# A graph layer's edge step in one round: two octets of tiles, one bank of partial products, one copy, one placing

## The chip, the cores and the metric

The kernel runs on one core of one Trainium2 chip. The metric is the device time of one execution in microseconds (us); lower is better. TensorE (PE) multiplies, VectorE (DVE) and ScalarE (ACT) work on rows, GpSimd (POOL) issues the gathers and scatters that go through an index, and SyncE (SP) issues the plain transfers.

## The reference

There are 12,500 nodes with 256 features and 212,500 edges, sorted by destination, so a node has 17 edges on average.

```
msgs = layernorm(x)[edge_src] * edge_weight[:, None]
agg  = segment_sum(msgs, edge_dst, num_segments=N_NODES)      # sorted
x = x + einsum('ni,oi->no', agg, W) + b
# then a feed-forward part on layernorm(x), with 8 experts:
H = gelu(xf @ W1 + b1);  probs = softmax(H @ Wg + bg);  assign = argmax(probs)
out += where(assign == e, probs[:, e] * (H @ Wd[e] + bd[e]), 0)   # for each e
```

All of it is in float32. The change concerns the sum over edges.

## The kernel before

The kernel has three stages. First the rows of x are normalised and stored to a table in HBM. Then comes the main loop, where nearly all of the time goes. At the end the nodes are sorted by expert, gathered, multiplied by their expert's weights and scattered to the output.

The edges are cut into tiles of 128, and a **step** is 16 tiles. There are 104 steps. GpSimd fetches the source rows with one indirect transfer for each tile (L387), 128 rows of 256 floats, into a ring of three sections of 16 tiles (`xring`). For each tile, VectorE builds a narrow matrix of 32 columns (`sel_narrow`), which has the edge's weight in the column of its destination, counted from the first destination of the tile. A product of that matrix and the fetched rows gives 32 rows of partial sums. Four tiles are a **quad**: their products stand in the four groups of 32 partitions of one bank of PSUM (`psR` or `psG`, in turn; `partial(q)`, L499). VectorE copies the bank to `parts` (L853). A second product with a matrix of zeros and ones (`place`, 64 columns) brings the rows to their places and transposes them (`place_quad(q)`, L507), and VectorE adds the outcome to a window of the sum `agg` in SBUF (`accumulate(q)`, L860). Each of these hand-overs is a semaphore: `s_edge_mm` from the partial products to the copy, `s_parts` from the copy to the placing, `s_placed` from the placing to the addition. So a step has four rounds, which are interleaved.

GpSimd runs ahead and is held back by the ring alone. Section g may be fetched when step g-3 no longer needs it, and this is asked twice for each section:

```
for j in range(STEP_TILES):
    if j % (STEP_TILES // 2) == 0:
        pool.wait_ge(s_edge_mm, g * STEP_TILES + STEP_TILES // 2 + j)
```

The first 8 gathers of a section wait for the first two quads of step g-3, the other 8 for the last two.

When all edges into a group of 512 nodes have been summed, after 4 or 5 steps, a **node group** is worked through: `messages` (L535, product with W, read by VectorE at L919), residual, norm and transposes, and, for the group before, the hidden layer (L557), its gelus on ScalarE (L450), transposes and the rows for the last stage. The order of steps and node groups is a table made on the chip; TensorE and VectorE both loop over it. For a step, VectorE runs `gather_step`, for a node group it runs `first_part` (L907 is its first copy, of `agg`) and `second_part`. There are 25 node groups.

If a tile spans 32 nodes or more, or a quad 64 or more, the step takes another branch (`wide == 1`). None of the 104 steps does with these edges.

## Time and profile before

| | us |
|---|---|
| median of 3 runs | 3659.85 (3650.84 to 3660.72) |
| profiled execution, its own time | 3686.61 |
| its span | 3684.6 |
| TensorE matmuls busy | 2061.4 (56%) |
| VectorE busy | 1151.1 (31%) |
| GpSimd busy | 1822.5 (49%) |
| ScalarE busy | 443.2 (12%) |

The span goes from the first to the last instruction of the profiled execution, and 2.0 us lie around it. A busy time says how much of the span an engine had an instruction in work; no engine is busy all the time here, so what matters is who waits for whom. In the views, PE is the matmuls, PEld the weight loads. A float32 matmul stands as two records, so four tiles show as x8, and the end of a matmul's record is modelled. "remote" is what the view names as the releaser of a wait when no instruction in the profile ended just before it.

### The profile page before, as it was taken

How to read it: one execution, taken by the hardware profiler on the slowest of the kernel's cores; microseconds unless marked ns; L12 is line 12 of the kernel's file. 1: busy time of each engine (PE TensorE's matmuls, PEld its weight loads, DVE VectorE, ACT ScalarE, POOL GpSimd, SP SyncE). 2: the span in 40 equal slices, each digit the busy share in tenths (PEclk: the TensorE clock that was granted, in tenths of full speed). 3: DMA queues.
4: the chain of work that ended last, by engine and by line, in shares of the span. 5: the costliest groups of instructions: out<-in, count | busy, mean ns of one | idle time of the engine just before them, and what ended most of it. 6: DMA issues, size and time to landing. Idle time of an engine off the chain costs nothing.

```text
span 3684.6 us, 40719 instructions
## 1 busy us (share of the span) xinstructions
PE 2061.4 (56%) x10526; PEld 1319.5 (36%) x10527; DVE 1151.1 (31%) x3507; ACT 443.2 (12%) x847; POOL 1822.5 (49%) x1988
## 2 busy tenths in 40 slices
PE   0134555455535554455445544555355548599998
PEld 0112332233323332233223322332233324488887
DVE  8121332233323332233223322332133224733332
ACT  5000000000000000000000000000000002043343
POOL 1656445644565445544664455444644540055554
PEclk9995666566656666566656656666566658799999
DMA  8323332333333332333233323332333231455554
GB/s 358 88 82 98 97 103 84 115 99 98 104 91 106 100 101 83 113 100 101 84 115 100 102 81 111 98 102 86 105 103 100 82 92 63 154 180 180 181 184 139
DMA packets 153598, 420.31 MB, mean 114 GB/s; under 512 B 33320, under 2 KB 67499, under 8 KB 150880
## 3 DMA queue, kind: packets, MB, share of 16 engines
q0 software_dynamic: 100032, 300.27, 27.6%
q1 hardware_dynamic: 53536, 119.73, 8.8%
q14 instruction: 23, 0.19, 0.0%
q8 instruction: 7, 0.11, 0.0%
HBM read 328.02 MB, written 92.82 MB: 114 GB/s over the span
## 4 chain that ended last, share of the span: by engine, by line
PE 38%; another core or an unknown queue 33%; issue 15%; DVE 7%; DVEq 5%; ACT 1%; DMA 0%; POOL 0%; ACTq 0%; POOLq 0%
PE psH L557 8%; PE psE L507 6%; PE psA L638 3%; PE psG L638 2%; PE psH L638 2%; PE psE L638 2%; PE psA L578 2%; PE psG L499 2%; PE psR L499 2%; PE psA L535 2%; DVEq L301 2%; DVE rows L942 1%; DVEq L295 1%; PE psG L564 1%
## 5 line engine op out<-in xcount | busy, mean ns | idle before, releaser
L387 POOL DMA_INDIRECT big<-xn_table,src_i x1664 | 1590.8, 956 | 1427.4 <-PE psG L499 620.8
L507 PE MATMUL psE<-place,parts 128*128 128x64 f32 x1664 | 450.8, 433 | 1015.3 <-DVE parts L853 778.4
L507 PEld LDWEIGHTS psE<-place,parts 128*128 128x128 f32 x1664 | 382.6, 324 | 1280.6 <-DVE parts L853 871.7
L557 PE MATMUL psH<-xn2T,w 128*128 128x512 f32 x800 | 427.9, 692 | 128.6 <-issue 64.5
L450 ACT ACTIVATE hidT<-psH,b 128x512 f32<-128x512 f32 x200 | 136.4, 687 | 2447.2 <-remote 1006.6
L499 PE MATMUL psR<-big,sel_narrow 128*32 128x256 f32 x1664 | 216.8, 613 | 289.4 <-issue 289.4
L557 PEld LDWEIGHTS psH<-xn2T,w 128*128 128x128 f32 x800 | 173.4, 223 | 347.8 <-issue 267.6
L860 DVE TENSOR_TENSOR big<-psE,big 128x128 f32 x416 | 121.2, 291 | 545.1 <-remote 294.3
L853 DVE COPY parts<-psR 128x256 f32<-128x256 f32 x208 | 88.0, 423 | 518.6 <-remote 461.2
L499 PE MATMUL psG<-big,sel_narrow 128*32 128x256 f32 x1664 | 217.6, 613 | 0.0
L864 DVE TENSOR_TENSOR place<-iota,shift_f 128x256 f32<-128x256 f32 x104 | 44.4, 427 | 447.7 <-issue 447.7
L401 POOL COPY stage<-rel_f 128x1 int32 (+1 forms) x105 | 19.2, 183 | 293.6 <-DVEq L1064 186.3
L942 DVE COPY rows<-psA 128x512 f32<-128x512 f32 x200 | 128.9, 686 | 94.8 <-PE psA L578 93.5
L853 DVE COPY parts<-psG 128x256 f32<-128x256 f32 x208 | 87.3, 420 | 225.5 <-remote 108.3
L499 PEld LDWEIGHTS psR<-big,sel_narrow 128*32 128x32 f32 x1664 | 41.7, 138 | 323.3 <-issue 311.0
L404 POOL DMA_INDIRECT rows<-row_table,stage x105 | 104.0, 991 | 86.9 <-POOL stage L401 85.2
L578 PE MATMUL psA<-ident,hidT 128*128 128x128 f32 x800 | 121.3, 285 | 18.3 <-DVE rows L942 18.1
L412 POOL DMA_INDIRECT out<-big,st_out x105 | 107.3, 1022 | 43.6 <-issue 30.4
L578 PEld LDWEIGHTS psA<-ident,hidT 128*128 128x128 f32 x800 | 84.1, 140 | 70.7 <-DVE rows L942 49.3
L535 PE MATMUL psA<-wt,aggs 128*128 128x256 f32 x400 | 98.2, 402 | 8.4 <-issue 8.4
L638 PE MATMUL psA<-big,hidT 128*128 x432 | 99.1, 383 | 0.0
L535 PEld LDWEIGHTS psA<-wt,aggs 128*128 128x128 f32 x400 | 82.5, 207 | 36.0 <-issue 24.8
(194 smaller groups left out, 2193.4 us busy)
## 6 DMA issues: line engine op xcount, KB each, us to landing
row_table<-rows SPq DMA_DIRECT2D x25, 2064.0 KB
big<-xn_table,src_i POOLq DMA_INDIRECT x1664
big<-in_x SPq DMA_DIRECT2D x10, 1280.0 KB, 17.5
xn_table<-big SPq DMA_DIRECT2D x10, 1280.0 KB, 12.9
big<-in_x SPq DMA_DIRECT2D x25, 512.0 KB
row_table<-big SPq DMA_DIRECT2D x25, 512.0 KB, 3.0
big<-in_Wd SPq DMA_DIRECT2D x8, 1024.0 KB, 12.0
hidT<-in_dstT SPq DMA_DIRECT2D x2, 840.0 KB, 30.3
```

The source lines that it names most:

```text
L387: nc.gpsimd.indirect_dma_start(out=xring[:, h * STEP_TILES + j, :], out_offset=None, in_=xn_dram[:, :], in_offset=bass.IndirectOffsetOnAxi ...
L412: nc.gpsimd.indirect_dma_start(out=out[:, :], out_offset=bass.IndirectOffsetOnAxis(ap=st_out[:, i:i + 1], axis=0), in_=ybuf[i], in_offset= ...
L450: nc.scalar.activation(hidT[:, c, :], psH[c % 2][:, :], ACT.Gelu, bias=b1[:, c:c + 1]).then_inc(s_gelu, 1)
L499: mm = nc.tensor.matmul(psQ[q % 2][j * LANES:(j + 1) * LANES, 0:C], sel_narrow[:, t, :], xring[:, t, :], start=True, stop=True)
L507: mm = nc.tensor.matmul(psE[q % 2][:, k * NARROW:(k + 1) * NARROW], parts[:, q % 2, k * P:(k + 1) * P], place[:, q, :], start=True, stop=True)
L535: mm = nc.tensor.matmul(psA[q // 2][:, (q % 2) * C:(q % 2 + 1) * C], aggs[:, k, q * P:(q + 1) * P], wt[:, k, :], start=(k == 0), stop=(k = ...
L557: mm = nc.tensor.matmul(psH[c % 2][:, :], w1[:, k, c * P:(c + 1) * P], xn2T[:, k, :], start=(k == 0), stop=(k == KC - 1))
L578: mm = nc.tensor.transpose(psA[i % 2][:, j * P:(j + 1) * P], hidT[:, 4 * half + j, q * P:(q + 1) * P], ident[:, :])
L638: mm = nc.tensor.matmul(psY2[i], hT2[i][:, c, :], wd[:, bass.ds(e8 + c, 1), :], start=(c == 0), stop=(c == HC - 1))
L853: nc.vector.tensor_copy(parts[:, q % 2, :], psQ[q % 2][:, 0:C]).then_inc(s_parts, 1)
L860: nc.vector.tensor_tensor(win, psE[q % 2][:, 0:KC * NARROW].rearrange("p (k n) -> p k n", k=KC), win, ALU.add).then_inc(s_acc, QUAD)
L942: nc.vector.tensor_copy(rows[:, q, C + half * 512:C + (half + 1) * 512], psA[i % 2][:, :]).then_inc(s_ev, 1)
```

## The change

Eight tiles, an octet, take the place of four, and a step has two octets. Within an octet, tiles 2j and 2j+1 share the 32 partitions of group j: their products are summed into the same place of PSUM (`start` on the even one, `stop` on the odd one). To keep them apart, the even tile's narrow matrix uses the columns from 0 and the odd one's the columns from 16 on (`iota2`), so that a tile may now span 15 nodes at most (the limit for the narrow branch was 31), and an octet 79 (`SPAN` = 80). Both octets stand in the two halves of one bank, `psR`. One copy of 128x512 takes them to `parts`, the placing is four matmuls with 80 columns into one bank, and two additions of 128x160 follow. Each hand-over happens once in a step.

```diff
-                    def partial(q):
-                        pe.wait_ge(s_narrow, g * 2 + q // 2 + 1)
-                        for j in range(QUAD):
...
-                        mm.then_inc(s_edge_mm, QUAD)
...
-                    partial(0)
-                    for q in range(1, QUADS):
-                        partial(q)
-                        place_quad(q - 1)
-                    place_quad(QUADS - 1)
+                    pe.wait_ge(s_narrow, g + 1)
+                    for o in range(OCTS):
+                        for odd in range(2):
+                            for j in range(OCT // 2):
+                                t = h * STEP_TILES + o * OCT + 2 * j + odd
+                                mm = nc.tensor.matmul(psQ[j * LANES:(j + 1) * LANES, o * C:(o + 1) * C],
+                                                      sel_narrow[:, t, :], xring[:, t, :],
+                                                      start=(odd == 0), stop=(odd == 1))
+                    mm.then_inc(s_edge_mm, STEP_TILES)
+
+                    pe.wait_ge(s_parts, g + 1)
+                    for o in range(OCTS):
                         for k in range(KC):
...
+                            at = (o * KC + k) * SPAN
+                            mm = nc.tensor.matmul(psW[:, at:at + SPAN], parts[:, o, k * P:(k + 1) * P],
+                                                  place[:, o, :], start=True, stop=True)
+                    mm.then_inc(s_placed, 1)
```

```diff
-                    copy_parts(0)
-                    narrow_onehots(g + 1, start, 0)
-                    copy_parts(1)
-                    narrow_weights(g + 1, start, 0)
-                    accumulate(0)
-                    copy_parts(2)
-                    narrow_onehots(g + 1, start, 1)
-                    accumulate(1)
-                    copy_parts(3)
-                    narrow_weights(g + 1, start, 1)
-                    accumulate(2)
-                    accumulate(3)
+                    dve.wait_ge(s_edge_mm, g * STEP_TILES + STEP_TILES + MM0)
+                    nc.vector.tensor_copy(parts[:, :, :], psQ[:, :].rearrange("p (o c) -> p o c", c=C)).then_inc(s_parts, 1)
+                    narrow_onehots(g + 1, start)
+                    dve.wait_ge(s_placed, g + 1)
+                    for o in range(OCTS):
+                        accumulate(o)
+                    narrow_weights(g + 1, start)
```

The tables made before the main loop change with it (`shift_f`, `octs_i`). GpSimd's code stays as it is. Its two waits of a section are now met by the same increment, of 16, at the end of a step's partial products.

On TensorE a step read like this before (rows in the order of the program; x4 are four matmuls; L505 is the wait for `s_parts`):

```order
L499 MATMUL psR<-big,sel_narrow 32x256 x4
L499 MATMUL psG<-big,sel_narrow 32x256 x4
L505 ISA
L507 MATMUL psE<-place,parts 128x64 x2
L496 REGISTER_ALU
L499 MATMUL psR<-big,sel_narrow 32x256 x4
L505 REGISTER_ALU
L507 MATMUL psE<-place,parts 128x64 x2
L499 MATMUL psG<-big,sel_narrow 32x256 x4
```

Now it reads like this, up to the branch that follows the step:

```order
L496 REGISTER_ALU
L501 MATMUL psR<-big,sel_narrow 32x256 x16
L510 MATMUL psE<-place,parts 128x80 x4
L495 UNCONDITIONAL_BRANCH
L513 COMPARE_AND_BRANCH
```

All sixteen partial products stand ahead of the first placing, and the eight placing matmuls of a step have become four.

On VectorE the first half of a step read like this before (L852 and L856 are the waits for `s_edge_mm` and `s_placed`):

```order
L864 TENSOR_TENSOR place<-iota,shift_f 128x256
L852 ISA
L853 COPY parts<-psR 128x256
L814 ISA
L814 TENSOR_TENSOR sel_narrow<-iota,rel_f 128x256
L852 REGISTER_ALU
L853 COPY parts<-psG 128x256
L823 ISA
L824 REGISTER_ALU
L824 TENSOR_TENSOR sel_narrow<-sel_narrow,w_f 128x256
L856 REGISTER_ALU
```

Now the whole step, up to its last instruction, reads:

```order
L864 TENSOR_TENSOR place<-iota,shift_f 128x160
L869 ISA
L870 COPY parts<-psR 128x512
L822 ISA
L822 TENSOR_TENSOR sel_narrow<-iota,rel_f 128x512
L858 REGISTER_ALU
L860 ISA
L860 TENSOR_TENSOR big<-psE,big 128x2x80
L858 REGISTER_ALU
L860 ISA
L860 TENSOR_TENSOR big<-psE,big 128x2x80
```

The weights of the next step's narrow matrices (L832, 128x512) moved behind the two additions.

## Rows read from the trace of the kernel before

**Rows 1.** The page: the span, and two groups (busy us, mean ns).

```profile
span 3684.6 us, 40719 instructions
...
L860 DVE TENSOR_TENSOR big<-psE,big 128x128 f32 x416 | 121.2, 291 | 545.1 <-remote 294.3
...
L942 DVE COPY rows<-psA 128x512 f32<-128x512 f32 x200 | 128.9, 686 | 94.8 <-PE psA L578 93.5
```

**Rows 2.** The waits of GpSimd: us in total, times, longest.

```profile
POOL big L387 <- PE psG L499: 620.8, 29, 30.2
...
POOL big L387 <- remote: 249.3, 81, 8.5
```

**Rows 3.** Timeline, one ordinary step (start us, duration, idle before and its releaser).

```profile
696.14 0.42 DVE L853 COPY parts<-psR 128x256 f32<-128x256 f32 x1 [7.72 <-remote]
696.47 0.94 POOL L387 DMA_INDIRECT big<-xn_table,src_i  x1 [3.27 <-remote]
...
696.62 1.12 PE L507 MATMUL psE<-place,parts 128*128 128x64 f32 x4 [11.70 <-DVE parts L853]
...
702.19 0.42 DVE L853 COPY parts<-psG 128x256 f32<-128x256 f32 x1 [1.86 <-PE psG L499]
...
706.20 1.08 PE L499 MATMUL psR<-big,sel_narrow 128*32 128x256 f32 x8 [2.41 <-issue]
...
707.05 1.08 PE L499 MATMUL psG<-big,sel_narrow 128*32 128x256 f32 x8
...
715.32 0.95 POOL L387 DMA_INDIRECT big<-xn_table,src_i  x1 [0.30 <-issue]
...
719.54 0.94 POOL L387 DMA_INDIRECT big<-xn_table,src_i  x1 [3.27 <-remote]
```

**Rows 4.** Timeline, the first step, while GpSimd gathers without a break.

```profile
106.23 1.08 PE L499 MATMUL psG<-big,sel_narrow 128*32 128x256 f32 x8
...
107.24 1.12 PE L507 MATMUL psE<-place,parts 128*128 128x64 f32 x4
...
125.79 0.42 DVE L853 COPY parts<-psG 128x256 f32<-128x256 f32 x1 [18.51 <-remote]
...
135.78 0.29 DVE L860 TENSOR_TENSOR big<-psE,big 128x128 f32 x1 [9.24 <-remote]
...
148.91 0.94 POOL L387 DMA_INDIRECT big<-xn_table,src_i  x1 [0.30 <-issue]
155.88 0.42 DVE L853 COPY parts<-psR 128x256 f32<-128x256 f32 x1 [19.81 <-remote]
```

**Rows 5.** Timeline, a node group after the restart of GpSimd at 719.54.

```profile
731.20 0.29 DVE L860 TENSOR_TENSOR big<-psE,big 128x128 f32 x1 [4.00 <-issue]
...
748.04 1.29 DVE L919 TENSOR_TENSOR big<-psA,big 128x512 f32<-128x512 f32 x2 [6.20 <-PE psA L535]
...
767.45 0.64 PE L499 MATMUL psR<-big,sel_narrow 128*32 128x256 f32 x8 [1.11 <-issue]
```

**Rows 6.** Timeline, the node group before that one.

```profile
609.07 0.94 POOL L387 DMA_INDIRECT big<-xn_table,src_i  x1 [3.22 <-PE psR L499]
...
615.02 0.29 DVE L860 TENSOR_TENSOR big<-psE,big 128x128 f32 x1 [2.00 <-PE psE L507]
...
622.50 3.62 PE L535 MATMUL psA<-wt,aggs 128*128 128x256 f32 x16
...
632.20 1.29 DVE L919 TENSOR_TENSOR big<-psA,big 128x512 f32<-128x512 f32 x2 [9.33 <-remote]
...
649.21 0.64 PE L499 MATMUL psR<-big,sel_narrow 128*32 128x256 f32 x8 [0.85 <-issue]
...
650.58 0.94 POOL L387 DMA_INDIRECT big<-xn_table,src_i  x1 [20.84 <-PE psG L499]
```

**Rows 7.** Timeline, first partial product after node groups: the first and the last of 23.

```profile
399.07 0.64 PE L499 MATMUL psR<-big,sel_narrow 128*32 128x256 f32 x8 [0.90 <-issue]
...
3060.94 0.64 PE L499 MATMUL psR<-big,sel_narrow 128*32 128x256 f32 x8 [0.90 <-issue]
```

More of the change, by code:

```diff
@@ L41 @@
 SECTIONS = 3
-QUAD = 4
-QUADS = STEP_TILES // QUAD
-NARROW = 64
+OCT = 8
+OCTS = STEP_TILES // OCT
+SPAN = 80
 LANES = 32
+HALF_LANES = LANES // 2
 TILES = NG * STEP_TILES
@@ L182, in build @@
         step_masks = selv[:, 0:2 * STEPS + 2 * NG]
-        span_tile, span_quad = (xn2T[:, a, 0:NG] for a in range(2))
+        span_tile, span_oct = (xn2T[:, a, 0:NG] for a in range(2))
         u = [selv[:, a * STEPS:(a + 1) * STEPS] for a in range(7)]
@@ L205, in build @@
         psR = psum("psR")
-        psQ = [psR, psG]
+        psQ, psW = psR, psE[1]
         s_ln_load = [sem(f"ln_load{c}") for c in range(LN_CHUNKS)]
@@ L723, in _ @@
+            nc.vector.tensor_scalar(fold[:, :], iota[:, 0:E], nhalf[:, 0:1], None, ALU.is_equal)
+            nc.vector.tensor_copy(iota2[:, 0, :], iota[:, 0:LANES])
+            nc.vector.tensor_scalar(iota2[:, 1, :], iota[:, 0:LANES], -float(HALF_LANES), None, ALU.add)
+            base_o = base_i[:, 0:TILES].rearrange("p (q j) -> p q j", j=OCT)
+            apart = slot_f[:, 0:TILES // OCT]
+            for j in range(OCT // 2):
                 rows_j = slice(j * LANES, (j + 1) * LANES)
-                o = nc.vector.tensor_tensor(shift_f[rows_j, :], base_q[rows_j, :, j], base_q[rows_j, :, 0],
+                nc.vector.tensor_tensor(shift_f[rows_j, :], base_o[rows_j, :, 2 * j], base_o[rows_j, :, 0],
+                                        ALU.subtract)
+                o = nc.vector.tensor_tensor(apart[rows_j, :], base_o[rows_j, :, 2 * j + 1], base_o[rows_j, :, 2 * j],
@@ L725, in _ @@
                                             ALU.subtract)
             tick(o)
-            nc.vector.tensor_scalar(shift_f[:, :], shift_f[:, :], nhalf[:, 0:1], None, ALU.add)
+            tick(nc.vector.scalar_tensor_tensor(out=shift_f[:, :], in0=apart, scalar=odd_lane, in1=shift_f[:, :],
+                                                op0=ALU.mult, op1=ALU.add))
+            nc.vector.tensor_scalar(shift_f[:, :], shift_f[:, :], lane, None, ALU.add)
             tick(nc.vector.tensor_tensor(rel_f[:, :], dst_i, base_i, ALU.subtract))
-            last_lane = newton[:, 1:2]
+            last_lane = newton[:, 3:4]
@@ L809, in _, with narrow_onehots, narrow_weights @@
             dve.wait_ge(s_weights, 16 * 7)
[L812 removed]
+            def narrow_onehots(g, start):
                 n = STEP_TILES // 2
                 nc.vector.tensor_tensor(
[L815 to L817 removed]
+                    selv[:, bass.ds(start, STEP_TILES * LANES)].rearrange("p (t h n) -> p t h n", h=2, n=LANES),
+                    iota2[:, :, :].unsqueeze(1).to_broadcast([P, n, 2, LANES]),
+                    rel_f[:, bass.ds(g * STEP_TILES, STEP_TILES)].rearrange("p (t h) -> p t h", h=2)
+                    .unsqueeze(3).to_broadcast([P, n, 2, LANES]),
                     ALU.is_equal).then_inc(s_narrow_eq, 1)
[L820 to L823 removed]
+            def narrow_weights(g, start):
+                both = selv[:, bass.ds(start, STEP_TILES * LANES)].rearrange("p (t n) -> p t n", n=LANES)
+                dve.wait_ge(s_narrow_eq, g + 1)
                 nc.vector.tensor_tensor(
                     both, both,
[L826 removed]
+                    w_f[:, bass.ds(g * STEP_TILES, STEP_TILES)].unsqueeze(2).to_broadcast([P, STEP_TILES, LANES]),
                     ALU.mult).then_inc(s_narrow, 1)
[L829 to L832 removed]
+            narrow_onehots(0, 0)
+            narrow_weights(0, 0)
             dve.wait_ge(s_xn_stored, 16 * LN_CHUNKS)
@@ L845, in gather_step @@
             def gather_step(g):
-                wide, *at, start = load_columns(quads_i[0:1, bass.ds(g, 1), :].rearrange("a b c -> a (b c)"), DVE,
+                wide, *at, start = load_columns(octs_i[0:1, bass.ds(g, 1), :].rearrange("a b c -> a (b c)"), DVE,
                                         (NS - 1) * SLOT + GROUP - 1)
@@ L895, in gather_step @@
                                                 win, ALU.add).then_inc(s_acc, 1)
-                    dve.sem_inc(s_parts, QUADS)
-                    for half in range(2):
-                        narrow_onehots(g + 1, start, half)
-                        narrow_weights(g + 1, start, half)
+                    dve.sem_inc(s_parts, 1)
+                    narrow_onehots(g + 1, start)
+                    narrow_weights(g + 1, start)
             def first_part(f, g, slot, spill):
```

93 lines of the change are left out of this document (36 added, 57 removed).

## The prediction

> **What bounds the kernel now.** I read the page first: in a span of 3684.6 us no engine is busy all the time [rows 1]. So I went to the waits. GpSimd waits 249 us in 81 pieces for "remote" and 621 us in 29 pieces for the products of psG [rows 2]. The timeline shows both. In an ordinary step GpSimd restarts at 696.47 and issues 16 gathers, one each 1.25 us (0.95 busy, 0.30 idle); the last starts at 715.32 and ends at 716.27; then it stands for 3.27 us and restarts at 719.54 [rows 3]. Steps follow at 23.07 us, of which gathers are 20. In the stand it waits for the first two quads of a step whose products ran from 706.20 to 708.13, 11.4 us earlier [rows 3]. So the work is done and the news of it is late.
>
> How late is seen in the first step, where gathers run without a break. The products of psG end at 107.31, and the copy that waits for them starts at 125.79, 18.5 us later. The placing issued next ends at 108.36; its addition starts at 135.78, 10.0 us after that copy. The next copy comes 20.1 us after the addition [rows 4]. These three stand for 8, 4 and 8 matmul records: 2.3, 2.5 and 2.5 us each. I read this so: while gathers run, TensorE's completions arrive in order and slowly, in proportion to the number of matmuls, and the backlog is released about 3.3 us after GpSimd's last gather. Just after a restart they are prompt: of the four rounds that follow 696.47, the last copy starts at 702.19 [rows 3]. Then the next step is caught. GpSimd cannot go on without the news, and the news comes when GpSimd stops: that makes the 23.07.
>
> The other stretch is the node group. With R for the restart before it, in one case (R = 719.54) the step's last addition ends at R+11.9, the products with W are read at R+28.5 and the next step's first product starts at R+47.9 [rows 5]. In the group before (R = 609.07) the last addition ends at R+6.2, the products end by their record at R+17.1 and are read at R+23.1, when the backlog is released, and the next first product starts at R+40.1 [rows 6]. From the read on, both run the same chain of VectorE and transposes, 17.0 and 19.4 us. In the timeline, ten of the 25 groups have the shape of the long case; others wait for the release alone. GpSimd restarts 1.37 us after the first product (650.58 against 649.21), after 20.84 us of idling [rows 6]: those are most of the 621 us.
>
> **The change part by part.**
>
> *Work on TensorE and VectorE.* The sixteen partial products keep their four rounds of 0.85 us (706.20 to 707.05, rows 3). The placing falls from 16 records to 8, and VectorE's copies, additions and builds go from 13 instructions to 6 longer ones. A copy of 128x512 takes 0.69, an addition of 128x128 0.29 [rows 1], so some 0.33 at 128x160. This lies beside the gathers' 20 us and is worth nothing in an ordinary step. If that cover were gone, it would be worth about 2 us a step.
>
> *The hand-overs.* A step has two completions of TensorE in place of eight, one after 32 records and one after 8. At R the sum's completion arrives; copy to R+0.7, placing (two times the 1.12 of rows 3) to R+2.9, two additions with their register work to R+3.9, the weights of the next narrow matrices to R+4.6. That last one is a new wait: the next step's products need it, where before they needed only work of mid-step. They could start at R+4.0 anyway (706.20 against the copy at 702.19, rows 3), so it costs 0.6 us under gathers: nothing. They end by their record at R+8.2, and their completion stands behind 40 records since the restart. Before, 32 records passed (4, 8, 4, 8, 4 and 4), and the next 16 were held to the release [rows 3]. So the 40th is held too. The restart comes at the same 23.07, and 71 of these intervals lie in the loop's 22 cycles below: 0 us. Bounds: from 20.0 (no stand) to 23.07 plus the 2.8 us of the slower rival.
>
> *GpSimd's credit.* The first 8 gathers of a section now wait for all 16 products rather than 8. Under gathers both come with the release. Only after a node group it shows, where products are prompt: the restart after the first product goes from 1.37 to between 1.4 and 2.7 us (two rounds or four, rows 6). I take 2.3.
>
> *The lead-in of a node group.* The last addition ends at R+3.9 rather than R+6.2 to R+11.9, since its placing completes in the prompt stretch. The hidden layer and the products with W start earlier, but under gathers: R+16 or so by the record, read at the release, R+23.1. The next first product is then at R+40.1, as in rows 6, for every group. That takes nothing from the short case and 7.8 us from the long one.
>
> *Sum.* Between the first products at 399.07 and 3060.94 there are 22 cycles and 93 steps in 2661.9 us [rows 7]. Of the 93 intervals 22 hold a node group. After: 22 x (2.3 + 40.1) + 71 x 23.07 = 933 + 1638 = 2571, so 91 us less. The node group ahead of 399 is a long one: 8 more. The first step (its copies wait through 48 gathers and 8 more, rows 4) and the last two steps, which run with no gathers, give an estimated 8 together. The tables ahead of the loop cost an estimated 1. Together 106 us: 3580.6 in place of the profiled execution's 3686.6, which stands 26.8 above the median of the runs; on the median 3554.
>
> By the Trainium skill (TensorE: Matmul & The Clock Gate, "The cost: per-tile semaphore tail") each increment adds 26.3 ns to a tail. By that the six saved ones are worth 0.16 us a step, 16 us in all, and none of it on GpSimd's path. Rows 4 show 10 to 20 us for one; the sum goes by the rows.
>
> **The rivals.**
>
> *A, the lateness goes by hand-over, not by matmul.* Then the one completion of a step's sum would come early in the 20 us, GpSimd would not stop, and an interval could fall to 20.0: 71 x 3.07 = 218 us more, at most 3336. With gathers never pausing, later completions take 10 to 20 us each [rows 4], two in series a step, so every other stand would remain: half of it, 3445. For it: six fewer events in a step. Against it: 18.5, 10.0 and 20.1 follow 8, 4 and 8 records.
>
> *B, slower: the release takes longer with a larger backlog.* A step's 32 records now stand behind the last gather, where 16 did. An ordinary release ends 3.27 us after the last gather's end; in the first step, after the long run, it was 155.88 against 149.85, 6.0 us [rows 3, 4]. If each release takes the 2.8 more, it costs at 71 stands and 22 node groups 93 x 2.8 = 260 us: 3814. It decides from 106/93 = 1.1 us each. Against it: the release at R+23.1 in rows 6 came with 16 products of W and 8 records of the hidden layer waiting.
>
> *C, nothing moves.* The placing of a step's last round would be late even at R+2.9, or the lateness has another origin than gathers, and node groups keep their two shapes: 3650. The Trainium skill (SBUF — State Buffer, "SBUF: two separate sides") says that a compute operation and a transfer cannot slow each other, save where GpSimd writes descriptors and VectorE holds their shared port. By it TensorE's completions could not hang on gathers. The trace bears this out badly: the stands end when the gathers do [rows 3].
>
> *D, the wide branch is taken.* With 17 edges a node a tile covers about 7.5 nodes (limit 15) and an octet 60 (limit 79), 19 nodes from it; the destinations are sorted and evenly drawn, so I leave out this case.
>
> **How the numbers follow.** Forecast 0.62, at 3554, its own range 3515 to 3595 (the lead-in may give half, or the last group's chain some us more). A 0.18, B 0.10, C 0.08; 0.02 for D and the rest, slower. Within 0.3% (11 us, about what a measurement of this kernel tells from no change) is C and a little of the weak end of the forecast: 0.09. Faster 0.79, slower 0.12. The range takes in A down to its half with something to spare and C at the top, and leaves out B: 3430 to 3665.
>
> **What would show it.** Right: restarts of GpSimd in ordinary steps still 23.1 us apart with a stand of 3.3 "remote"; after a restart one copy, 8 placing records and two additions done by R+4; the products with W read at R+23 in nearly all groups and the next first product at R+40; the count of stands about 90. Wrong: intervals near 20 (A); stands of 5 us or more (B); additions before a node group still at R+6 to R+12 (C). What would make the forecast wrong above all is that a release isn't tied to the gathers' stop as I read it, for then GpSimd's pace changes at every one of the 71 intervals.

## The result, and the profile after

The changed kernel took 3709.89 us (median of 4 runs, 3703.74 to 3718.55) against 3659.07 for kernel before: ratio 1.0145, 95% interval 1.0117 to 1.0173. It is 1.4% slower, where 2.9% faster was forecast. Its profiled execution has a span of 3712.0 us. Times are medians of all runs; ratios leave out runs that lie over 1.5% above the fastest of their kernel, which only e13 and e14 have.

The page of the kernel after: span, chain of work by engine, and the groups of the gathers, the copy and the addition (busy us, mean ns, then idle time and what ended it).

```profile
span 3712.0 us, 36326 instructions
...
another core or an unknown queue 52%; PE 29%; DVE 7%; issue 6%; DVEq 4%; ACT 1%; DMA 0%; POOL 0%; ACTq 0%; POOLq 0%
...
L389 POOL DMA_INDIRECT big<-xn_table,src_i x1664 | 1594.2, 958 | 1466.9 <-PE psR L501 747.2
...
L870 DVE COPY parts<-psR 128x512 f32<-128x512 f32 x104 | 71.7, 690 | 798.2 <-remote 748.6
L860 DVE TENSOR_TENSOR big<-psE,big 128x160 f32 x208 | 67.6, 325 | 680.1 <-remote 535.2
```

The instructions have the sizes that the prediction gave them (0.69 and 0.33 us), and no engine is busier. What grew is idle time, and over half of the chain is put down to "unknown": waits that no record of work ends.

The waits of the kernel after, GpSimd's first, then those of VectorE and TensorE (us in total, times, longest).

```profile
POOL big L389 <- PE psR L501: 747.2, 28, 37.1
...
POOL big L389 <- remote: 159.0, 46, 7.1
...
DVE parts L870 <- remote: 748.6, 64, 39.6
DVE big L860 <- remote: 535.2, 38, 19.9
...
PE psR L501 <- DVE sel_narrow L832: 194.6, 28, 19.9
```

Against [rows 2], GpSimd's waits for "remote" fell from 249.3 to 159.0 us and those for the products rose from 620.8 to 747.2. The last row is new: 28 times a step's products wait up to 19.9 us for the narrow weights, which VectorE now makes behind the additions.

The timeline of the kernel after, an ordinary step (start us, duration, idle before and its releaser).

```profile
679.69 0.69 DVE L870 COPY parts<-psR 128x512 f32<-128x512 f32 x1 [13.73 <-remote]
679.93 0.94 POOL L389 DMA_INDIRECT big<-xn_table,src_i  x1 [1.68 <-remote]
...
680.44 2.00 PE L510 MATMUL psE<-place,parts 128*128 128x80 f32 x8 [12.12 <-DVE parts L870]
...
689.15 0.79 DVE L860 TENSOR_TENSOR big<-psE,big 128x160 f32 x2 [8.17 <-remote]
689.86 0.68 DVE L832 TENSOR_TENSOR sel_narrow<-sel_narrow,w_f  x1
...
690.60 3.64 PE L501 MATMUL psR<-big,sel_narrow 128*32 128x256 f32 x32 [8.16 <-issue]
...
699.15 0.95 POOL L389 DMA_INDIRECT big<-xn_table,src_i  x1 [0.30 <-issue]
703.96 0.69 DVE L870 COPY parts<-psR 128x512 f32<-128x512 f32 x1 [5.52 <-remote]
704.19 0.94 POOL L389 DMA_INDIRECT big<-xn_table,src_i  x1 [4.09 <-remote]
```

The stand was only 1.68 us, and the placing's completion is 6.7 us late (end 682.44, addition 689.15), in the stretch that the prediction took to be prompt. The products follow 0.74 us behind the start of the weights (689.86), which stand behind the late addition, and their news again comes only after the last gather.

The timeline of the kernel after, from there through the node group.

```profile
706.93 0.79 DVE L860 TENSOR_TENSOR big<-psE,big 128x160 f32 x2 [1.69 <-issue]
...
708.38 3.64 PE L501 MATMUL psR<-big,sel_narrow 128*32 128x256 f32 x32 [1.68 <-issue]
...
720.61 0.69 DVE L870 COPY parts<-psR 128x512 f32<-128x512 f32 x1 [9.46 <-remote]
721.36 2.00 PE L510 MATMUL psE<-place,parts 128*128 128x80 f32 x8 [9.34 <-DVE parts L870]
...
741.83 0.79 DVE L860 TENSOR_TENSOR big<-psE,big 128x160 f32 x2 [19.93 <-remote]
...
750.19 0.69 DVE L901 COPY aggs<-big 128x1024 f32 x1 [6.96 <-issue]
...
753.66 4.07 PE L531 MATMUL psA<-wt,aggs 128*128 128x256 f32 x16
...
757.95 1.29 DVE L913 TENSOR_TENSOR big<-psA,big 128x512 f32<-128x512 f32 x2 [5.57 <-PE psA L531]
...
777.41 1.93 PE L501 MATMUL psR<-big,sel_narrow 128*32 128x256 f32 x32 [1.16 <-issue]
779.64 0.95 POOL L389 DMA_INDIRECT big<-xn_table,src_i  x1 [35.51 <-PE psR L501]
```

Here is the loss. The products end at 712.02 and VectorE's copy, which waits for their completion, starts at 720.61, inside the 20 us of gathers. It isn't VectorE that is slow to look: in the trace's record of semaphore updates, the step of `s_edge_mm` itself stands at 720.59. So GpSimd has leave for the next section and gathers on for 40 us, from 704.19 to 744.13. The placing, issued at 721.36, falls in the middle of that run: its addition comes 18.5 us after its end, the node group starts late, and GpSimd, out of leave, stands for 35.51 us. In [rows 6] it was 20.84, which is among the shortest of before; the 23 long stands average 26.4 us there and 31.2 us here.

ScalarE hears late as well: the hidden layer's matmuls that start at 725.41 end by their record at 731.71, and the gelu that reads them starts at 749.35.

This table counts the same things for the profiles of the kernels named below. "Short" are stands of GpSimd in the edge part from 1.25 to 12 us, "long" those above (node groups); "late" is the number of copies and additions that VectorE starts over 5 us after the end of the last matmul's record, with the mean lateness of all (for the additions less some 0.2 us of register work ahead of them).

```
kernel (gathers each, us)   short stands   long stands    copies late   additions late
before (1.25)               84,  264 us    23,  608 us    171 of 416    57 of 416
after (1.25)                43,  184 us    23,  718 us    63, mean 7.7  37, mean 5.0
e9  after again (1.25)      38,  172 us    23,  687 us    64, mean 7.9  38, mean 4.2
e15 half rows (1.25)        42,  190 us    23,  684 us    65, mean 7.6  37, mean 4.8
e16 weights first (1.25)    38,  178 us    23,  587 us    44, mean 8.4  39, mean 3.1
e1  pause (1.25)            88,  248 us    23,  572 us    70, mean 8.4  41, mean 2.9
e10 64 records (1.25)       79,  257 us    22,  527 us    47, mean 4.8   0, mean 0.0
e3  spaced (1.34)           47,  131 us    22,  411 us    41, mean 8.3  15, mean 2.2
e12 pause of 8 (1.25)      207,  508 us     0             1,  mean 1.4   0, mean 0.4
e11 spaced (1.44)            0              0             6,  mean 1.8   0, mean 0.0
e8  64 records (1.25)        0              0             0,  mean 0.3   0, mean 0.0
```

Short stands went from 264 to 184 us (80 less, where the prediction had 0), long ones from 608 to 718 (110 more, where it had about 100 less). The net of 30 us is about the 27 us by which the span grew; two smaller terms nearly cancel, 13 us more in gaps under 1.25 us and in the gathers themselves, and 15 us less behind the last gather.

The rows of before need care: VectorE works in the order of its program, so an addition also counts as late when it stands behind a late copy. Counted from when VectorE had come free, 10 of before's 416 additions and 65 of its 416 copies are over 5 us late.

The trace shows the long runs directly. Between stands, GpSimd of before makes 90 runs of 16 gathers, 15 of 8, 2 of 24, and one of 56 at the start. After makes 31 of 16, 35 of 32, and one of 48 at the start. From the start of the last 16 gathers ahead of a node group to the next first product, before takes 45.6 us on average. After takes 48.5: in the 8 groups whose last run had 16 gathers 43.0, in the 15 with a run of 32 it is 51.5.

### The profile page after: what moved, and what is told of

The parts are those of the page before. It is cut to its first block, busy times and chain, and to the rows that moved or that the text cites. A ratio compares the mean times of both kernels' runs of the same rounds, so it can differ in the third digit from the quotient of the medians.

```text
span 3712.0 us, 36326 instructions
## 1 busy us (share of the span) xinstructions
PE 1776.3 (48%) x9694; PEld 1145.8 (31%) x9695; DVE 977.8 (26%) x2788; ACT 442.6 (12%) x847; POOL 1826.0 (49%) x1988
## 3 DMA queue, kind: packets, MB, share of 16 engines
q0 software_dynamic: 100032, 300.27, 27.6%
## 4 chain that ended last, share of the span: by engine, by line
another core or an unknown queue 52%; PE 29%; DVE 7%; issue 6%; DVEq 4%; ACT 1%; DMA 0%; POOL 0%; ACTq 0%; POOLq 0%
PE psH L553 9%; PE psA L634 3%; PE psE L634 2%; PE psG L634 2%; PE psH L634 2%; PE psA L574 2%; PE psA L531 2%; DVEq L297 2%; DVE rows L936 1%; PE psG L560 1%; DVE stats L690 1%; ACT hidT L452 1%; PE psE L510 1%; DVEq L303 1%
## 5 line engine op out<-in xcount | busy, mean ns | idle before, releaser
L389 POOL DMA_INDIRECT big<-xn_table,src_i x1664 | 1594.2, 958 | 1466.9 <-PE psR L501 747.2
L553 PE MATMUL psH<-xn2T,w 128*128 128x512 f32 x800 | 455.8, 729 | 329.4 <-ACT hidT L452 270.8
L510 PE MATMUL psE<-place,parts 128*128 128x80 f32 x832 | 183.1, 391 | 882.5 <-DVE parts L870 801.7
L501 PE MATMUL psR<-big,sel_narrow 128*32 128x256 f32 x3328 | 339.5, 579 | 522.4 <-issue 327.9
L510 PEld LDWEIGHTS psE<-place,parts 128*128 128x128 f32 x832 | 162.2, 290 | 961.3 <-DVE parts L870 872.9
L501 PEld LDWEIGHTS psR<-big,sel_narrow 128*32 128x32 f32 x3328 | 138.7, 156 | 667.5 <-issue 457.8
L870 DVE COPY parts<-psR 128x512 f32<-128x512 f32 x104 | 71.7, 690 | 798.2 <-remote 748.6
L860 DVE TENSOR_TENSOR big<-psE,big 128x160 f32 x208 | 67.6, 325 | 680.1 <-remote 535.2
L864 DVE TENSOR_TENSOR place<-iota,shift_f 128x160 f32<-128x160 f32 x104 | 33.9, 326 | 408.4 <-issue 408.4
L634 PE MATMUL psE<-big,hidT 128*128 x416 | 94.2, 379 | 0.0
L634 PE MATMUL psH<-big,hidT 128*128 x416 | 94.1, 379 | 0.0
```

Of the source, the lines that this page charges most:

```text
L389: nc.gpsimd.indirect_dma_start(out=xring[:, h * STEP_TILES + j, :], out_offset=None, in_=xn_dram[:, :], in_offset=bass.IndirectOffsetOnAxi ...
L501: mm = nc.tensor.matmul(psQ[j * LANES:(j + 1) * LANES, o * C:(o + 1) * C], sel_narrow[:, t, :], xring[:, t, :], start=(odd == 0), stop=(od ...
L510: mm = nc.tensor.matmul(psW[:, at:at + SPAN], parts[:, o, k * P:(k + 1) * P], place[:, o, :], start=True, stop=True)
L553: mm = nc.tensor.matmul(psH[c % 2][:, :], w1[:, k, c * P:(c + 1) * P], xn2T[:, k, :], start=(k == 0), stop=(k == KC - 1))
L634: mm = nc.tensor.matmul(psY2[i], hT2[i][:, c, :], wd[:, bass.ds(e8 + c, 1), :], start=(c == 0), stop=(c == HC - 1))
```

## The experiments

The eighteen kernels ran in five sittings, each with kernel before beside it: e1 to e4, e5 to e8, e9 to e12, e13 to e16, e17 and e18. Kernel before took 3663, 2824, 3592, 3661 and 2823 us in them. That is the largest effect of the study, and it is no work of mine: in the second and fifth sitting no completion was late, in the others they were. The chips' numbers on record are 14, 10, 4, 1 and 4. Number 4 had late completions in sitting 3 and none in sitting 5, 27 minutes later, so if the number names the same chip, the chip alone doesn't decide it. What does isn't told by these runs. Ratios hold within a sitting.

**Sitting 1 (before 3663 us).** e1 bounds the run of gathers:

```diff
                     ).then_inc(s_gath[h], 16)
+                pool.wait_ge(s_gath[h], (g // SECTIONS + 1) * STEP_TILES * 16)
```

> Kernel after, but GpSimd waits at the end of each section until that section's 16 gathers have landed, so it stops once every 16 gathers and a burst is never longer than 20 us. Theory 1 (what costs is the unbroken 40-us burst: completions inside it come 12 to 18 us late and the node group behind it idles 30 to 37 us): bursts of 20 us everywhere, ordinary intervals 22.9 to 23.3 us, the last addition ahead of a node group at R+4 to R+5, GpSimd's idle at a node group 21 to 24 us; about 3555 to 3600 us. Theory 2 (lateness in proportion to the matmul records): the stops were there anyway, so time of after or a little longer, 3700 to 3740, with the last addition of a step still late. Rival: the pause comes on top of the stands that are there, 66 stands more of 3 us at most: up to 3850 us.

Measured: 3631.71 us, ratio 0.9917 (0.9893 to 0.9940), so 2.3% under the ratio of after. Its waits:

```profile
POOL big L389 <- PE psR L502: 572.2, 23, 28.1
...
POOL big L389 <- remote: 133.7, 40, 5.2
...
POOL big L389 <- DMA big<-xn_table,src_i: 100.5, 48, 3.3
```

The last row is the added pause, 100 us. It is more than paid for: the waits at node groups fell from 747 to 572 us, the longest from 37.1 to 28.1. That fits theory 1: the 40-us run ahead of a node group costs, and without it the way from the last 16 gathers to the next first product takes 42.2 us in place of 48.5. The size fell short (3555 to 3600 was expected): 41 additions are still over 5 us late.

e2 counts 8 after each octet, so that each has a completion:

```diff
-                    mm.then_inc(s_edge_mm, STEP_TILES)
+                        mm.then_inc(s_edge_mm, OCT)
```

> Kernel after, but each octet's partial products count 8 on the semaphore that GpSimd and VectorE wait for, where after counts 16 once at the end. Two completions for 32 records in place of one; the copy still waits for both. Theory 1 (a completion waits for a gap in the gathers, whatever it counts): the first 8 gathers are freed 0.9 us earlier, at node groups only; 3690 to 3712 us. Theory 2 (per record): the same, 3690. Rival 3 (lateness per completion event): the second one comes one more service time later, some 2.5 to 5 us per step where it is late; 3730 to 3800 us.

Measured: 3712.82 us, ratio 1.0126 (1.0099 to 1.0153), as after. So the coarser leave of GpSimd isn't the cause of the loss. The trace isn't the same, though: 41 runs have 24 gathers, short stands are 284 us (after: 184) and long ones 618 (after: 718). Their total is 902 us in both. How the stands divide into short and long is thus no measure of the loss by itself, and the total is.

e3 and e4 put a small memset and its wait between gathers, in after and in before; e5, e6, e11, e13, e14 and e17 are the same with other widths (e6 and e13 with one buffer, and the wait ahead of the memset):

```diff
                     ).then_inc(s_gath[h], 16)
+                    k = g * STEP_TILES + j
+                    nc.gpsimd.memset(pad[:, k % 2, 0:128], 0.0).then_inc(s_pad, 1)
+                    if k:
+                        pool.wait_ge(s_pad, k)
```

> Kernel after, with a small memset and a semaphore wait between every two gathers of the edge part, so that gathers come about every 1.6 us in place of 1.25. If gathers come faster than something they share with TensorE's completions can serve (arrivals are quantised at about 1.4 us when gathers have stopped, so a service time above 1.25 us): completions become prompt, under 3 us late, stands vanish, the section takes 16 x 1.6 = 25.6 us and 104 of them plus tables, node lead-ins and the routed part give 3350 to 3600 us. If any running gather holds completions back however they are spaced: stands stay about 3 us, intervals 28.5 us, 4000 us or more.

> Kernel before with the same spacing of gathers. If spacing makes completions prompt, it lies within 1% of the spaced version of after, 3350 to 3620 us. If lateness is tied to running gathers whatever their spacing: 28.5 us an interval, 4000 us or more. If it goes per matmul record, before (48 records a step against 40) gains as much from the spacing as after does.

Measured: the gathers came each 1.34 us, not 1.6. e3: 3508.56 us, ratio 0.9568 (0.9537 to 0.9598). e4: 3724.03, ratio 1.0147 (1.0110 to 1.0183). Slower issue, by 0.09 us a gather (1664 of them, 150 us), took after from 1.0145 to 0.9568 of before's time, and made before slower. In e3, products that end 3 to 9 us into a run of gathers are heard 1.8 us late on average (10.8 in after for an age of 6 to 9 us), those that end past 12 us still some 20; placings that end past 12 us are 7.1 us late. The expectation that before gains alike was wrong: 134 of its 416 additions are over 5 us late in e4 (57 in before), or 25 (10 in before) from when VectorE had come free. Before spreads eight hand-overs over the whole section, which is a likely reason and not tested.

**Sitting 2 (before 2824 us).**

> Kernel after with a memset of 128x256 between gathers, so one gather about each 1.43 us (1.25 in after, 1.34 with the memset of 128x128). Theory S (completions of TensorE share something with the gathers that has room for one gather in about 1.3 to 1.4 us; a backlog builds up with the age of the burst): completions late by under 3 us at any age of a burst, bursts over 100 us, total stands under 400 us, 3250 to 3450 us. Rival G (a small pause in each gather's cycle lets one completion through, its length does not matter): lateness as with 1.34 us, some 20 us for completions that fall in at an age above 12 us, and 0.09 x 1664 = 150 us of issue more: 3550 to 3660 us.

> Kernel after with a memset of 128x512 between gathers, so one gather about each 1.63 us. Theory S: everything prompt, GpSimd becomes the bound with 104 sections of 26 us; 0.2 x 1664 = 330 us more of issue than with 1.43 and at most the stands less; 3400 to 3550 us, with stands in total under 200 us. Rival G: 3800 us or more.

> Kernel after, but GpSimd waits for the landing of its gathers after each 8 of them, so bursts are 10 us with stops of about 2 us: a mean of 1.5 us a gather, between the spaced versions, but given as stops and not as spacing. Theory S: between the two stops a backlog of at most 10 us builds, which drains in a stop; completions up to some 8 us late, and a section of 24 us: 3480 to 3620 us. Rival L (it is the length of the unbroken burst alone): same as spaced gathers at this mean rate, under 3450 us. Rival M (a stop of 2 us is too short to release anything; a release needs 3.3 us): as the version with one pause a section plus 2 us a section, 3800 us.

> Kernel after, but each partial product is made as two matmuls of 128 columns, so a step has 64 records of TensorE for them in place of 32, with the same two completions. Theory of the prediction (2.5 us of lateness for each record): 32 records more a step, the lateness of the copies doubles or the stands grow by tens of us; over 3900 us. Theory S or any theory by completion or by age of the burst: within 0.7% of after, 3690 to 3735 us.

e7 waits for the landing of the gathers after each 8; e8 splits each product in two:

```diff
-                        for odd in range(2):
+                        for c, odd in ((0, 0), (0, 1), (1, 0), (1, 1)):
...
-                                mm = nc.tensor.matmul(psQ[j * LANES:(j + 1) * LANES, o * C:(o + 1) * C],
-                                                      sel_narrow[:, t, :], xring[:, t, :],
+                                mm = nc.tensor.matmul(psQ[j * LANES:(j + 1) * LANES, o * C + c * P:o * C + (c + 1) * P],
+                                                      sel_narrow[:, t, :], xring[:, t, c * P:(c + 1) * P],
```

Measured: 3135.75, 3489.08, 3202.72 and 2810.26 us (ratios 1.1106, 1.2358, 1.1334, 0.9951 with 0.9935 to 0.9968). Since nothing was late here, these tell only what the kernels cost then. The waits of e8 on GpSimd:

```profile
POOL big L389 <- issue: 581.3, 1663, 75.1
```

No gather waits for a product: 1664 gathers run through, and the loop takes 2116 us from first to last. Where completions are prompt, the edge step is hidden altogether, and even with doubled matmuls the changed kernel is 0.5% faster than before. As tests of the theories e5 to e8 were void, and three of them were repeated.

**Sitting 3 (before 3592 us).**

> Kernel after, unchanged, beside kernel before on whichever chip is given: in the four runs before this one, kernel before took 2824 us, where it took 3660 us in the first eight. On a chip of the first kind: 3700 to 3720 us against 3660. On one of the second kind, where no completion of TensorE was late in the traces and GpSimd never stopped: the step's shape lies beside the gathers, so the gathers' 104 x 16 x 1.27 us bound the loop in both kernels; 2805 to 2825 us against 2824, from the two last steps and the node group behind the gathers, where eight hand-overs become two.

> Kernel after with 64 matmul records for a step's partial products in place of 32, two completions a step as in after. On a chip with late completions: by the theory of the prediction (2.5 us a record) over 3900 us; by completion or by age of the burst, 3690 to 3735 us. On a chip without them: within 0.7% of after.

> Kernel after with gathers each 1.43 to 1.46 us. On a chip without late completions it took 3136 us, all issue of GpSimd. On a chip with them: theory S (gathers and completions share a server that a gather keeps busy for some 1.3 to 1.4 us) says completions late by under 3 us at any age and a time within 3% of that 3136 us; rival G (20 us late past the age of 12 us, as with gathers each 1.34 us) says 3550 us or more.

> Kernel after with a stop of 2.1 us after each 8 gathers. Without late completions it took 3203 us. With them: theory S says that a backlog of at most 10 us drains in part in each stop, completions up to 8 us late, 3250 to 3500 us; the rival that a stop of 2 us releases nothing says 3650 us or more.

Measured: after 3668.97 us, ratio 1.0186 (1.0139 to 1.0233), the same loss as in the result. e10: 3596.45, ratio 1.0007 (0.9988 to 1.0025), faster than after by 2.0% with twice the matmuls. e11: 3138.75, ratio 0.8736 (0.8706 to 0.8765). e12: 3259.55, ratio 0.9066 (0.9034 to 0.9098). The timeline of e10, a stand:

```profile
693.93 0.62 PE L501 MATMUL psR<-big,sel_narrow 128*32 128x128 f32 x2 [0.33 <-issue]
...
699.49 0.94 POOL L389 DMA_INDIRECT big<-xn_table,src_i  x1 [0.30 <-issue]
703.24 0.69 DVE L870 COPY parts<-psR 128x512 f32<-128x512 f32 x1 [15.80 <-remote]
703.47 0.94 POOL L389 DMA_INDIRECT big<-xn_table,src_i  x1 [3.04 <-remote]
...
703.98 2.00 PE L510 MATMUL psE<-place,parts 128*128 128x80 f32 x8 [9.43 <-DVE parts L870]
...
706.21 0.79 DVE L860 TENSOR_TENSOR big<-psE,big 128x160 f32 x2 [1.69 <-PE psE L510]
```

Sixty-four records stand behind the gathers. The copy starts 2.8 us after the last gather's end and GpSimd restarts after 3.04, where it was 3.27 with sixteen records [rows 3]. So the lateness is not made of TensorE's records, and the theory of the prediction falls. Since the products now end too late to be heard inside the 20 us, GpSimd stops after every section, the placing is issued at a real stop, and none of the 104 additions is late: the step that the prediction described. Ordinary intervals are 23.1 us on average, the way from the last 16 gathers to the next first product takes 41.8 us (41.0 to 42.6) in every group, and GpSimd's credit is 2.25 us. Against the one profile of before that there is (3684.6 us, another sitting), its span of 3592.8 is 92 us shorter. Beside before in its own sitting it is level, for there before took 3592 us and not 3659. What made before faster there isn't known, since this sitting has no profile of it.

The timeline of e11, in the middle of its one run of gathers of 2439 us without a stand:

```profile
1223.18 2.10 PE L507 MATMUL psR<-big,sel_narrow 128*32 128x256 f32 x32 [1.32 <-issue]
...
1230.05 0.69 DVE L876 COPY parts<-psR 128x512 f32<-128x512 f32 x1 [2.75 <-remote]
...
1230.79 2.00 PE L516 MATMUL psE<-place,parts 128*128 128x80 f32 x8 [5.50 <-DVE parts L876]
1233.02 0.79 DVE L866 TENSOR_TENSOR big<-psE,big 128x160 f32 x2 [1.68 <-PE psE L516]
```

With 1.44 us between gathers the copy is up to 5.5 us late, 1.8 on average, and the addition not at all, however long the run. Rival G is ruled out. Theory S has the time right and the lateness roughly: it said under 3 us at any age, and 6 copies are over 5. The time is that of e5 (3136 us), where nothing was late to begin with: GpSimd's issue alone.

**Sitting 4 (before 3661 us).** e13 and e14 are spaced by 1.45 us (before) and 1.39 us (after); e15 gathers 512 bytes a row instead of 1024; e16 moves the weights:

```diff
-                        out=xring[:, h * STEP_TILES + j, :], out_offset=None, in_=xn_dram[:, :],
+                        out=xring[:, h * STEP_TILES + j, 0:P], out_offset=None,
+                        in_=xn_dram.rearrange("n (h c) -> (n h) c", h=2),
```

```diff
+                    narrow_weights(g + 1, start)
                     dve.wait_ge(s_placed, g + 1)
                     for o in range(OCTS):
                         accumulate(o)
-                    narrow_weights(g + 1, start)
```

> Kernel before with a memset of 128x256 between gathers, one gather each 1.44 us, as the spaced kernel of after that took 3139 us. If completions are prompt then, the edge step of before hides beside 23 us of gathers as that of after does, and the time is 3139 to 3160 us (the last two steps and the last node group cost some us more). If before's eight hand-overs of a step load what the gathers leave free more than after's two do, its completions stay 5 to 15 us late and it takes 3300 to 3650 us.

> Kernel after with a memset of 128x192, one gather each 1.39 us. Theory S with a service of under 1.39 us: prompt, and GpSimd bound: 3139 less 1664 x 0.05 = 3050 us. With a service of 1.39 to 1.44 us: a backlog grows slowly, some late completions at ages above 30 us: 3100 to 3350 us. On a chip without late completions 3050 us.

> Kernel after, but each gather fetches 128 pieces of 512 bytes in place of 128 rows of 1024 (the second half of each row in the ring stays what it was, and the pieces are not the right ones, so the output is not the reference's); the number of descriptors and of gathers, their issue time and all work on TensorE and VectorE stay. If it is the gathers' data that completions queue behind: completions prompt, GpSimd never stops, 2800 to 2850 us on any chip. If it is the descriptors or their making: late as in after, 3600 to 3720 us.

> Kernel after, but VectorE makes the weights of the next step's narrow matrices ahead of its wait for the placing, as soon as the one-hots are there; the next step's partial products then need not wait for a late placing. If that new wait is part of the loss (28 long waits of the products for these weights, 195 us): the products of the next step run at an age of 5 to 8 us of the burst in each step, the additions ahead of a node group are late as before, and the time falls by 30 to 100 us against after. If the loss lies in the lateness of the last addition ahead of node groups alone: within 0.7% of after. By the prediction (it costs 0.6 us under gathers, nothing): the same as after.

Measured: e13 3376.27 us, ratio 0.9202 (0.9126 to 0.9278); e14 3381.36, ratio 0.9102 (0.9030 to 0.9174); e15 3687.42, ratio 1.0064 (1.0039 to 1.0088); e16 3594.27, ratio 0.9776 (0.9717 to 0.9835).

e15: the gathers' bytes fell from 300 to 191 MB with the routed part's, and the lateness stayed (65 copies and 37 additions late, as in after). It isn't the bytes that completions queue behind, nor the packets, which fell from 100,032 to 73,408 on GpSimd's queue. The 128 pieces of a gather, or their making by GpSimd, are left, and which of the two isn't told. e15 is also the nearest thing to after in this sitting, which has no run of after. Against it, e16 is 93 us or 2.5% faster; by the ratios of after in other sittings (1.0145 and 1.0186) the gain would be larger. First e15's wait of the products for the weights, then a timeline of e16 ahead of a node group:

```profile
PE psR L502 <- DVE sel_narrow L833: 173.1, 20, 19.3
```

```profile
675.23 0.69 DVE L870 COPY parts<-psR 128x512 f32<-128x512 f32 x1 [6.14 <-remote]
675.97 2.00 PE L510 MATMUL psE<-place,parts 128*128 128x80 f32 x8 [5.32 <-DVE parts L870]
676.64 0.69 DVE L832 TENSOR_TENSOR sel_narrow<-sel_narrow,w_f  x1
679.50 3.63 PE L501 MATMUL psR<-big,sel_narrow 128*32 128x256 f32 x31 [1.53 <-issue]
683.20 0.79 DVE L860 TENSOR_TENSOR big<-psE,big 128x160 f32 x2 [5.87 <-remote]
...
707.70 0.69 DVE L870 COPY parts<-psR 128x512 f32<-128x512 f32 x1 [18.05 <-remote]
```

The 173.1 us (e15) have no such row in e16: the next products start at 679.50, ahead of the late addition at 683.20. The long runs remain (short stands 178 us against 190), and the gain is in the long stands, 587 us against 684. So the new wait is a cause of its own, of about 90 us. With it gone the change is 2.2% faster than before (1.7 to 2.8%), with GpSimd's gathers as they were; the other kernels under before's time (e1, e3, e11, e12, e14) hold the gathers back.

e13 lies in the range of its second case (3300 to 3650: completions stay late), e14 by its median above all of its ranges, the highest of which ended at 3350. Their runs scatter (3330 to 3436 and 3327 to 3430 us). In e13 before's copies were 3.3 us late on average, 129 of 416 over 5 us. No kernel of after was spaced by 1.44 us in this sitting, so whether the sitting or the eight hand-overs of before made the difference to e11 isn't told.

**Sitting 5 (before 2823 us).** e17 is e16's order with gathers each 1.44 us, e18 the same order with e7's pause after each 8.

> Kernel after with the weights ahead of the wait for the placing, and gathers each 1.44 us. If the two causes account for the loss: GpSimd's issue alone sets the time, 3125 to 3145 us on any chip, with no stand of over 1.5 us. If completions stay 5 us late or more on this chip and a node group then outruns GpSimd's lead of three sections: 3200 to 3400 us.

> Kernel after with the weights ahead of the wait for the placing, and GpSimd waiting for the landing of its gathers after each 8. The same with the weights behind took 3260 us beside a kernel before of 3592, and 3203 us where no completion was late. With both mended: 3200 to 3240 us, stands of 2.1 us only. If the weights' place matters only in unbroken bursts of 20 us or more: as before, 3240 to 3280 us on a chip with late completions.

Measured: 3145.00 us, ratio 1.1142 (1.1123 to 1.1161), and 3199.90 us, ratio 1.1336 (1.1317 to 1.1355). Nothing was late in this sitting, so they say nothing on the two causes together; they repeat that with prompt completions spacing and stops only cost. Against e5 and e7 the order of the weights makes +9 and -3 us. The combined version wasn't seen where completions are late.

## Why the prediction was wrong, step by step

- **What bounds the kernel: right.** GpSimd's issue plus its waits for late news of TensorE's work. Where the news is prompt, before takes 2824 us, so lateness costs it over 800 us.
- **"Slowly, in proportion to the number of matmuls": wrong.** e10 doubled the records and its releases took 2.8 us; e2 doubled the products' completions and took as long as after. What the lateness follows is the gathers: how close they are (1.25, 1.34, 1.44 us), how long they have run, and how long the stand before was (the late placing of 682.44 came 2.5 us into a run, behind a stand of only 1.68 us). The 18.5, 10.0 and 20.1 us of [rows 4] were three places in one long run, not 8, 4 and 8 records.
- **"So the 40th is held too": the step that failed first.** It gave every ordinary interval 23.07 us. In after, products that end 6 to 9 us into a run are heard 6.3 to 15.3 us late (10.8 on average), often just inside the section (720.61). Short stands fell from 84 to 43 and by 80 us, and 35 runs of gathers became 40 us long. That is the effect which rival A named (GpSimd does not stop), though not by its rule of one delay for each hand-over; I had it at 0.18 and priced it as a gain of 218 or half of it.
- **"The last addition ends at R+3.9 ... for every group": wrong, and the larger term.** It supposed a real stop ahead of each placing. Without one, the placing falls in the middle of 40 us of gathers (addition at 741.83, 37.6 us after the restart at 704.19). Long stands went up by 110 us where 99 less was forecast. The way from the last 16 gathers to the next first product, 40.1 us by the forecast and 45.6 before, became 51.5 behind a run of 32 and 43.0 behind one of 16. Rival A's gain and this loss have the same origin, which neither the forecast nor the rivals put together. e1 shows it by taking the long runs away: ratio 1.0145 to 0.9917. Where nothing was heard inside a run (e10), the way took 41.8 us in every group, so this term was near right for a step that really ends in a stand; with the credit, 22 groups at 44.1 us are an estimated 64 us under before's 47.0, where 91 were forecast.
- **"It costs 0.6 us under gathers: nothing": wrong.** The cover named for the new wait was prompt additions. With 37 of 104 late, the weights and the next products wait with them: 194.6 us in 28 waits, about 90 us of time by e16 against e15.
- **The credit of GpSimd after a node group:** 2.23 us from first product to restart (777.41 to 779.64), forecast 2.3. Right. So are the prices of the copy and the addition. The two ends of the loop gave more than the 8 us forecast: from the last gather on, after takes 15 us less.
- **Rival B** (releases take longer with a larger backlog) was wrong on what makes the backlog. Releases do take longer after a longer run: in e9 about 3.0 us after 20 us of gathers, 5.4 after 40, 6.8 after 62 (and where a stand of 1.6 us cut one short, the next was 4.4: together again twice 3.0); in e10, with twice the records, 3.1 after 20. Rival D did not occur, and C's "nothing moves" was no better.

Both runs of after agree on the loss (1.0145 and 1.0186). Shown are the two causes, the long runs and the new wait; what isn't shown is their sum in one kernel under late completions, nor why completions are late at all.

## What to carry to other kernels

When a wait ends long after the work that it waits for, find out first what the lateness follows (records, completions, the other engine's pace), for a change that removes stops can lengthen the very condition that makes news late, and lose behind it more than the stops had cost. Merging rounds puts more behind each late piece of news: keep work that the next round needs (here the weights) ahead of the wait and not behind it. And time the kernel before in every sitting: here the same code differed by 30% between sittings, and a remedy worth 13% in one cost 11% in another.

## What the runs showed of the hardware

- Completions of TensorE reach VectorE, ScalarE and GpSimd 6 to 20 us late while GpSimd issues indirect gathers of 128 rows each 1.25 us, in the result and three sittings. In e8 (sitting 2), with the same pace and a single run of 1664 gathers, the mean was 0.3 us; in sitting 5 it was 0.2, with gathers spaced or stopped.
- The age of the run counts. In after, work that ended in the first 6 us of a run was heard 0.8 us late on average (66 cases), at 6 to 9 us 10.8 (38, all of them products). In before, counted from when VectorE had come free, it was 0.3 us in the first 3 us, 0.7 at 3 to 6, 2.4 at 6 to 9 and 3.3 at 9 to 12. It isn't all: at 6 to 9 us the products are 10.8 us late in after and 5.6 in e16.
- The gathers themselves aren't late. In after, a gather's last packet ends 1.6 us after its instruction at the start of a run and 1.5 us at its 32nd gather, and the last update of a section's `s_gath` stands within 0.4 us of the last packet. So in the same microseconds the landings are told promptly and TensorE's work is not.
- The way back is prompt: TensorE issues the placing 0.05 to 0.1 us after the copy's end. The Trainium skill (SBUF — State Buffer, "SBUF: two separate sides") lets compute and transfers slow each other only by the shared port of VectorE and GpSimd. It speaks of access to SBUF and not of semaphores, so these runs don't contradict it; they show that TensorE's completions can hang on gathers all the same (before: 3659 against 2824 us).
- An estimate from e9: 16 more gathers in a run (20 to 40 us) lengthen the release by 5.4 - 3.0 = 2.4 us, 0.15 us a gather. So whatever is shared would need some 1.40 us for a gather; from 40 to 62 us the release grows by 1.4 us only, which gives 1.34. The spaced runs lie around that: 1.34 us is too close (e3), 1.39 helps in part (e14), 1.44 is wide enough for after in sitting 3 (e11), and 1.45 not quite for before in sitting 4 (e13). What is shared isn't the moving of the data, by the packets above.
- A backlog of 2 to 5 us does not by itself explain a completion that is 18 us late. Why completions fare so much worse than the queue stays open.
- Halving the bytes left it as it was (e15), and stops of 2.1 us in the median after each 8 gathers make nearly all completions prompt (e12: copies 1.4 us late on average), at a mean pace of 1.5 us.
